# One transformer block with warped attention and two-of-eight experts on one core: ScalarE's distances in slices, another order of experts, transposes and norms, and another order of the first loads

## The reference

```python
mod = (silu(c) @ wmod).reshape(16, 6, 1, 128)           # sa, ca, ga, sb, cb, gb
ga, gb = (2*(g >= 0) - 1) * maximum(abs(g), 0.25)       # for g = ga and gb
h = layernorm(x) * (1 + ca) + sa
wave = silu(h @ wave_w.T + wave_b)                      # 2 x 8 values a row
freq  = mean(sigmoid(wave[0])) * 15 + 1                 # one a row
phase = mean(tanh(wave[1])) * 16
w = silu(h @ kernel_w.T + kernel_b)[..., :33]           # 8 heads x 33 taps
pos = clip(row + (tap - 16) * freq + phase, 0, 255)
g = h at floor(pos), h at floor(pos) + 1, interpolated  # 8 heads x 16 values
x = x + ga * silu(sum(g * w over taps) @ out_w.T)
h = layernorm(x) * (1 + cb) + sb
mask = the two largest of h @ router_w.T + router_b     # of 8 experts
x = x + gb * sum over experts of mask * (h @ expert_w[e] + expert_b[e])
```

## Time and profile before

| | |
|---|---|
| device time, median of 3 runs | 381.81 us |
| lowest, highest | 379.74, 382.86 us |
| profiled execution, device time | 381.84 us |
| its span in the profile | 380.1 us |
| mean granted clock of TensorE | 0.847 |
| activation table loads | 1 |

### The profile page before, as it was taken

One profiled execution on the slowest core, in us unless ns is written; L12 is line 12 of the kernel. 1 busy time (PEld: TensorE's weight loads), 2 busy tenths in 40 slices (PEclk: granted clock), 3 DMA queues, 4 the chain that ended last, 5 costly groups with the idle time before them and its releaser, 6 DMA issues.

```text
span 380.1 us, 5110 instructions
## 1 busy us (share of the span) xinstructions
PE 276.8 (73%) x1720; PEld 189.1 (50%) x1720; DVE 278.9 (73%) x584; ACT 237.2 (62%) x650; POOL 50.3 (13%) x64
## 2 busy tenths in 40 slices
PE   7873861989188928887498919894798479679796
PEld 4333430756065427644375517543564366358474
DVE  6678956995589962999469964999199949950623
ACT  2557755777588557867677758856676646575301
POOL 5102004500320031000310031002100300001100
PEclk9955855599669986999599988999699969899689
DMA  6600000010003000130004000400013001200001
GB/s 220 162 1 1 2 0 0 0 57 1 1 2 125 2 0 1 48 93 2 0 1 141 0 0 2 131 10 2 0 25 116 0 3 47 94 0 2 28 0 41
DMA packets 11871, 12.91 MB, mean 34 GB/s; under 512 B 1139, under 2 KB 10694, under 8 KB 11078
## 3 DMA queue, kind: packets, MB, share of 16 engines
q1 hardware_dynamic: 11108, 12.05, 10.5%
q10 hardware_dynamic: 738, 0.55, 0.5%
HBM read 10.45 MB, written 2.15 MB: 33 GB/s over the span
## 4 chain that ended last, share of the span: by engine, by line
PE 48%; ACT 29%; issue 7%; DVE 7%; POOL 7%; DMA 1%; SPq 0%; ACTq 0%; POOLq 0%; DVEq 0%
PE pT L898 12%; PE pE L986 11%; PE pR L878 7%; ACT A L470 6%; ACT xn L378 5%; POOL rs L309 5%; ACT c L456 4%; PE pY L912 4%; ACT xn L352 4%; PE pY L922 2%; PE pR L873 2%; ACT hT L400 2%; DVE AT L723 2%; PE pX L938 2%; DVE T L691 2%
## 5 line engine op out<-in xcount | busy, mean ns | idle before, releaser
L898 PE MATMUL pT<-early,AT 128*128 128x128 f32 x512 | 79.1, 304 | 21.2 <-ACT A L470 13.2
L470 ACT ACTIVATE A<-pT 128x512 f32<-128x512 f32 x128 | 70.6, 595 | 21.8 <-PE pT L898 21.4
L691 DVE COPY_PREDICATED T<-mask,T 128x672 f32<-128x672 int16 (+11 forms) x54 | 82.8, 1533 | 1.0
L898 PEld LDWEIGHTS pT<-early,AT 128*128 128x128 f32 x512 | 61.7, 155 | 36.1 <-ACT A L470 24.1
L723 DVE TENSOR_TENSOR AT<-T,c 128x2064 f32<-128x2064 f32 x32 | 72.4, 2302 | 7.0 <-ACT c L459 6.9
L986 PE MATMUL pE<-hm,late 128*128 128x256 f32 x240 | 65.7, 434 | 0.0
L986 PEld LDWEIGHTS pE<-hm,late 128*128 128x128 f32 x240 | 51.5, 220 | 10.6 <-issue 1.3
L938 PE MATMUL pX<-early,xn 128*128 128x128 f32 x32 | 8.7, 416 | 58.3 <-ACT xn L378 58.3
L307 POOL TENSOR_SCALAR ve<-sq 128x4 f32<-128x4 f32 (+1 forms) x18 | 7.7, 426 | 300.5 <-ACT xn L352 294.3
L378 ACT ACTIVATE xn<-x,nm,rs 128x128 f32<-128x128 f32 x64 | 26.4, 480 | 31.5 <-POOL nm L311 31.5
L938 PEld LDWEIGHTS pX<-early,xn 128*128 128x128 f32 x32 | 5.4, 206 | 61.6 <-ACT xn L378 61.1
(11 more groups left out here) (131 smaller groups left out, 363.0 us busy)
## 6 DMA issues: line engine op xcount, KB each, us to landing
mkb<-mask_rows SPq DMA_DIRECT2D x6, 1024.0 KB, 5.2
x<-in_x SPq DMA_DIRECT2D x7, 256.0 KB, 7.5
out<-x SPq DMA_DIRECT2D x7, 256.0 KB, 5.0
late<-in_late SPq DMA_DIRECT2D x1, 592.0 KB, 5.3
mkb<-mask_rows SPq DMA_DIRECT2D x1, 512.0 KB, 5.2
wmod<-in_wmod ACTq DMA_DIRECT2D x1, 384.0 KB, 4.2
early<-in_early SPq DMA_DIRECT2D x1, 278.0 KB, 4.4
x<-in_x SPq DMA_DIRECT2D x2, 128.0 KB, 3.6
```

The lines of the kernel that those rows point to most:

```text
L470: nc.scalar.activation(A[b][:, m, 2 * j:2 * j + 2, :].rearrange("p h l -> p (h l)"), pT[k % 2][:, :], ACT.Copy).then_inc(a_A, 1)
L691: nc.vector.copy_predicated(rows[:, :, :, j0:j1], spread(mask[:, k, 0:w, j0:j1], [P, w, H, j1 - j0], 2), rows[:, :, :, j0 + (1 << bit):j1 ...
L898: ins = nc.tensor.transpose(pT[k % 2][:, c0:c0 + P], AT[:, 2 * b + i, 2 * j + a, m * P:(m + 1) * P], ident)
```

## The change

- **c in slices.** `front_c(n, r0, r1)` now issues the slices r0 to r1 of the six, each with its own increment of a_abs, and `front_fall` the fall. Slices 0, 1 and 2 stand ahead of `mid_ao`, of row 0 and of `mid_y`; slices 3 to 5 between rows 1 and 2; the fall between rows 2 and 3.
- **ScalarE's loop.** The A copies of the second image are ahead of `front_hT`. The rows are issued one by one. `stats2` is right behind `front_wave`, then `front_hs`, `front_u`, `norm2`, `back_h2T`, `stats1`.
- **TensorE's loop.** The first half of the second image's A transposes is ahead of `front_xT`. Row 0 is ahead of `mid_y`, row 1 ahead of `mid_gate`, rows 2 and 3 behind it. Both images' experts are ahead of `back_x2T`.
- **VectorE's loop.** `residual` is ahead of the second image's `masked`.
- **The tail.** `front_c(LAST)` is behind all A copies of unit 7 and its fall behind `mid_ao`; the first `masked` of unit 6 is ahead of `spread_out(LAST, 0)`; unit 6's experts of the first image are ahead of `mid_gate(LATE)`, those of the second directly behind `mid_y(LAST)`; norm2(LATE) is behind the gate of the last unit, norm2(LAST) ahead of back_mk(LATE).
- **The start.** The identity is a pack of its own, `first`. SP loads x of unit 0, first, proj, x of unit 1, early, bits, experts, and behind hT of unit 0 the x of unit 2, late, rb and the rest. wmod comes in two parts, chunks 0 and 1 and, behind ScalarE's silu, chunks 2 to 5. The modulation has two parts, both into pL: the second one's matmuls stand behind the rows of iteration -1, its VectorE steps and the gates at the end of iteration 0. The bias parts are made ahead of the wait for the identity. `expert_parts` stands in iteration -1 behind the statistics of unit 1, `selectors`, its last step, at the end of iteration 0.

The core of the diff:

```diff
             load_x(0)
+            sp.dma_start(packs["first"][:, :], t["first"]).then_inc(d_first, 16)
+            sp.dma_start(proj[:, 0:NW], t["proj"][:, 0:NW]).then_inc(d_proj, 16)
+            sp.dma_start(proj[:, NW:NW + H], t["proj"][:, NW:NW + H]).then_inc(d_proj, 16)
+            sp.dma_start(proj[:, NW + H:NW + 2 * H], t["proj"][:, NW + 32:NW + 40]).then_inc(d_proj, 16)
+            load_x(1)
             sp.dma_start(packs["early"][:, :], t["early"]).then_inc(d_early, 16)
             sp.dma_start(bits[:, :, :], t["bits"].rearrange("p (k j) -> p k j", j=NGRID)).then_inc(d_bits, 16)
-            load_x(1)
             sp.dma_start(packs["experts"][:, :], t["experts"]).then_inc(d_exp, 16)
+
+            sp.wait_ge(a_hT, 1)
+            load_x(2)
             sp.dma_start(packs["late"][:, :], t["late"]).then_inc(d_late, 16)
             sp.dma_start(rb[:, :], t["rb"].rearrange("(a e) -> a e", a=1).to_broadcast([P, E])).then_inc(d_late, 16)
-            for n in range(2, NU):
+            for n in range(3, NU):
                 load_x(n)
...
-            act.dma_start(wmod[:, :], t["wmod"]).then_inc(d_wmod, 16)
+            act.dma_start(wmod[:, 0:2 * C], t["wmod"][:, 0:2 * C]).then_inc(d_wmod[0], 16)
...
             nc.scalar.activation(scT[:, :], cT[:, :], ACT.Silu).then_inc(a_silc, 1)
-            act.dma_start(proj[:, 0:NW], t["proj"][:, 0:NW]).then_inc(d_proj, 16)
-            act.dma_start(proj[:, NW:NW + H], t["proj"][:, NW:NW + H]).then_inc(d_proj, 16)
-            act.dma_start(proj[:, NW + H:NW + 2 * H], t["proj"][:, NW + 32:NW + 40]).then_inc(d_proj, 16)
+            act.dma_start(wmod[:, 2 * C:6 * C], t["wmod"][:, 2 * C:6 * C]).then_inc(d_wmod[1], 16)
...
-            def front_c(n):
+            def front_c(n, r0, r1):
                 w = tiles(n)
-                act.wait_ge(v_near, n + 1)
-                if n > 0:
-                    act.wait_ge(v_mult, LT * before(n))
+                if r0 == 0:
+                    act.wait_ge(v_near, n + 1)
+                    if n > 0:
+                        act.wait_ge(v_mult, LT * before(n))
                 cells = c[:, 0:w, :].rearrange("p a (j r) -> p a j r", r=BLK)
-                for r in range(BLK):
-                    ins = nc.scalar.activation(cells[:, :, :, r], near[:, 0:w, :], ACT.Abs, bias=off[:, r:r + 1])
-                ins.then_inc(a_abs, 1)
-                act.wait_ge(a_abs, n + 1)
+                for r in range(r0, r1):
+                    nc.scalar.activation(cells[:, :, :, r], near[:, 0:w, :], ACT.Abs, bias=off[:, r:r + 1]).then_inc(a_abs, 1)
+
+            def front_fall(n):
+
+                w = tiles(n)
+                act.wait_ge(a_abs, BLK * (n + 1))
                 nc.scalar.activation(c[:, 0:w, :], c[:, 0:w, :], ACT.Relu, bias=1.0, scale=-1.0).then_inc(a_c, 1)
...
             for i in range(-2, LAST):
+                second(i, -1, mid_A, 1)
                 run(i, 1, front_hT)
-                second(i, -1, mid_A, 1)
+                run(i, 0, front_c, 0, 1)
                 run(i, -1, mid_ao)
+                run(i, 0, front_c, 1, 2)
+                run(i, 1, front_row, 0)
+                run(i, 0, front_c, 2, 3)
                 run(i, -1, mid_y)
                 run(i, -1, mid_gate)
-                run(i, 1, front_row, 0)
                 run(i, 1, front_row, 1)
+                run(i, 0, front_c, 3, BLK)
+                run(i, 1, front_row, 2)
+                run(i, 0, front_fall)
+                run(i, 1, front_row, 3)
                 run(i, 1, front_wave)
+                run(i, -1, stats2)
                 run(i, 1, front_hs)
-                run(i, 0, front_c)
-                run(i, -1, stats2)
+                run(i, 1, front_u)
                 run(i, -1, norm2)
-                run(i, 1, front_u)
                 run(i, -1, back_h2T)
                 run(i, 2, stats1)
                 run(i, -2, back_moe)
                 run(i, 0, mid_A, 0)
                 run(i, -1, back_mk)
                 run(i, 2, norm1)
-            mid_A(LATE, 1, (0,))
-            front_c(LAST)
-            mid_A(LATE, 1, (1,))
+            mid_A(LATE, 1)
+            front_c(LAST, 0, BLK)
             mid_ao(LATE)
+            front_fall(LAST)
             mid_y(LATE)
             mid_gate(LATE)
             mid_A(LAST, 0)
             stats2(LATE)
             mid_ao(LAST)
-            norm2(LATE)
             mid_y(LAST)
             mid_gate(LAST)
+            norm2(LATE)
             back_h2T(LATE)
             back_moe(LATE - 1)
             stats2(LAST)
+            norm2(LAST)
             back_mk(LATE)
-            norm2(LAST)
             back_h2T(LAST)
             back_mk(LAST)
...
             def projection_parts():
-                dve.wait_ge(d_early, 16)
                 dve.wait_ge(d_kb, 48)
                 dve.wait_ge(g_zero, 3)
-                parts_on_partitions(kbl[:, :], kbr[:, :], kbs, kbt, kbp[:, :], ident[0:NP, 0:NP], v_kbp)
+                parts_of(kbl[:, :], kbr[:, :], kbs, v_kbp)
+
+            def projection_rows():
+                dve.wait_ge(d_first, 16)
+                on_partitions(kbs, kbt, kbp[:, :], ident[0:NP, 0:NP], v_kbp)
...
+            def modulation(part):
+
+                ks = slice(0, 2) if part == 0 else slice(2, 6)
+                dve.wait_ge(t_mod, part + 1)
+                nc.vector.tensor_copy(modT[:, ks, :].rearrange("p k b -> p (k b)"),
+                                      pL[:, ks.start * B:ks.stop * B]).then_inc(v_modT, 1)
+                dve.wait_ge(v_modT, 2 * part + 1)
+                nc.vector.tensor_scalar(modT[:, 3 * part + 1, :], modT[:, 3 * part + 1, :], 1.0, None, ALU.add).then_inc(v_modT, 1)
...
-            for i in range(-2, LAST):
+            stats1(0)
+            projection_parts()
+            modulation(0)
+            projection_rows()
+            for i in range(-1, LAST):
                 run(i, 0, network, range(0, 2))
-                if i < 0:
-                    run(i, 2, stats1)
-                if i == -2:
-                    projection_parts()
-                    modulation()
-                    gates()
+                if i == -1:
+                    stats1(1)
+                    expert_parts()
                 run(i, 0, sum_ends)
                 run(i, 0, network, range(2, 4))
                 run(i, -2, masked, 0)
                 run(i, 0, network, range(4, 5))
+                run(i, -1, residual)
                 second(i, -2, masked, 1)
-                run(i, -1, residual)
                 run(i, 0, network, range(5, 6))
                 run(i, 1, line)
                 run(i, 1, ends_of)
                 run(i, 1, products)
                 run(i, -2, total)
                 if i == 0:
-                    expert_parts()
+                    modulation(1)
+                    gates()
...
             sum_ends(LAST)
+            masked(LATE - 1, 0)
             spread_out(LAST, 0)
-            masked(LATE - 1, 0)
             residual(LATE)
             masked(LATE - 1, 1)
...
+            def modulation(part, ks):
+                pe.wait_ge(d_wmod[part], 16)
+                for k in ks:
+                    ins = mm(pL[:, k * B:(k + 1) * B], wmod[:, k * C:(k + 1) * C], scT[:, :], start=True, stop=True)
+                ins.then_inc(t_mod, 1)
+
+            modulation(0, range(0, 2))
+            pe.wait_ge(d_first, 16)
...
             for i in range(-2, LAST):
+                second(i, -1, mid_A, 1, 0)
                 run(i, 1, front_xT)
-                second(i, -1, mid_A, 1, 0)
                 second(i, -1, mid_A, 1, 1)
                 second(i, -1, mid_attend, 1, 0)
                 second(i, -1, mid_attend, 1, 1)
+                run(i, 1, front_row, 0)
                 run(i, -1, mid_y)
-                run(i, 1, front_row, 0)
+                run(i, 1, front_row, 1)
                 run(i, -1, mid_gate)
-                run(i, 1, front_row, 1)
+                run(i, 1, front_row, 2, 3)
+                if i == -1:
+                    modulation(1, range(2, 6))
                 run(i, 1, front_hb)
                 if i == -1:
                     warm_up(9)
                 run(i, -2, back_experts, 0)
+                second(i, -2, back_experts, 1)
                 run(i, -1, back_x2T)
-                second(i, -2, back_experts, 1)
                 run(i, -1, back_logits)
                 run(i, 0, mid_A, 0, 0)
                 run(i, -2, back_out)
             mid_attend(LATE, 1, 0)
             mid_attend(LATE, 1, 1)
             mid_y(LATE)
+            back_experts(LATE - 1, 0)
             mid_gate(LATE)
             mid_A(LAST, 0, 0)
             mid_A(LAST, 0, 1)
             mid_attend(LAST, 0, 0)
             mid_attend(LAST, 0, 1)
-            back_experts(LATE - 1, 0)
             mid_y(LAST)
+            back_experts(LATE - 1, 1)
             back_x2T(LATE)
```

49 lines of the change are left out of this document (24 added, 25 removed).

## The result

The changed kernel takes 331.7 us (median of 4 runs, 330.22 to 334.54) beside 381.5 us for the kernel before on the same chip (379.74 to 382.86): a ratio of 0.871, interval 0.863 to 0.878. It is faster by 50 us. The profiled execution took 330.67 us, its span is 328.9 us, and its mean granted clock 0.886 where that of before is 0.847.

What follows compares the result with a forecast made beforehand. A ring of waits through ScalarE and TensorE, no single engine. Savings 21.2 (iterations 3 to 6), 4.9 (2), 5.5 (7), 7 (1), 1.7 (start), 2.1 (tail), 42.4 in all, off 381.8 gave 339 us; range 325 to 358.

Steps and rivals of the forecast that it cites:

- (a): Loop, second image's A copies ahead of hT, first A transposes ahead of xT: saves 1.0 us an iteration (0 to 1.3).
- (b): ScalarE's loop, c in slices and hs behind the statistics: aoT to statistics 10.71 to 7.5 us, gain 3.2 (2 to 3.9).
- (c): ScalarE's loop, u ahead of the second norm, inside its wait for GpSimd: gain 0.7 us an iteration (0.4 to 1.0).
- (d): TensorE's loop, both images' experts ahead of the x2 transposes, filling the 8.08 us hole: waits of 1.3 us go.
- (e): TensorE between x2 transposes and first A copies: pauses may bring half clock, costing 0.9 us an iteration (0 to 2.6).
- GpSimd caught by both AT products: Rival: second norm's power instruction held under VectorE's products, norm2 3.3 us later in five iterations; 356 us, chance 0.10.
- VectorE's floor: VectorE's own work, 33.4 us an iteration, below which no reordering of the other engines can go.
- Start: Loads, identity, bias and modulation reordered: 0.6 us from these edits, 1.7 together with iteration 0 (-1 to 3).
- Tail: After the loop: c out of the A copies, experts and last norm moved; saves 2.1 us in all (0 to 4).
- Slices that cost what they save: Rival: rows wait for slices of c and TensorE for rows, (a) and (b) give 1; 358 us, chance 0.08.
- Half clock all round the loop: Rival: TensorE at 1.2 GHz through the loop becomes the bound, 48.7 us an iteration; 426 us, chance 0.03.
- Clock and GpSimd both kind: Rival: no half clock in the loop and the second norm waits only for the experts; 329 us, chance 0.17.

Runs made afterwards that it cites:

- e6: Kernel after with hT and the x transposes again ahead of the second image's A copies and transposes; 339.5 us, 0.899.
- e4: Kernel after with c whole (six slices and the fall) behind the tanh values, ahead of the second norm's statistics; 359.2 us, 0.950.
- e5: Kernel after with u behind the second norm again; 334.4 us, 0.886.
- e1: Kernel before with one edit, both images' experts ahead of the x2 transposes; 378.5 us, 0.998.
- e3: Kernel after with the second image's experts behind the x2 transposes again; 343.8 us, 0.910.
- e7: Kernel after with unused matmuls on zeros in TensorE's pauses, up to four ahead of the logits, eight ahead of the second pair of A transposes; 326.5 us, 0.863.
- e10: Kernel after with the tail of the kernel before on all three engines; 331.2 us, 0.875.
- e8: Kernel after with the first norm's sums ahead of h2T on ScalarE, the squares behind it; 325.5 us, 0.860.
- e9: Kernel after with one added wait: VectorE begins an iteration's first AT product only after GpSimd's three second-norm steps; 325.7 us, 0.859.
- e2: Kernel before with c cut into three pieces of two slices, its fall behind the second row; 363.5 us beside 378.9.
- e12: Kernel after with first-norm sums ahead of h2T, four zero-matmul fills per pause from unit 3, and VectorE's AT products waiting for GpSimd; 320.2 us, 0.846.
- e11: Kernel after with the loads, modulation, bias and expert parts of the kernel before; 333.5 us, 0.882.

## Why the prediction was right, and where its sizes were off

The mechanism and the sign held, and 331.7 lies in the range of 325 to 358. The forecast of 339 was 7 us too slow; in the profiled executions -42.4 was forecast and -51.2 came. The missing 8.8 lie in iterations 3 to 6 (5.6), start (2.3), tail (1.4), iterations 7 (0.8) and 1 (0.5), less iteration 2 (1.8 the other way). Of a full iteration, 5.3 was forecast and 6.56 came in iteration 5, whose parts can be read off and ScalarE's rows above:

**(a) 1.0.** From the end of the first image's attention to aoT's start it is 8.41 before and 7.12 after: 1.3. e6 takes the part away and loses 1.2. Right.

**(b) 3.2.** From aoT's start to the statistics' start 7.5 was forecast; it is 187.07 - 179.89 = 7.18, so 3.5. Right in size, and e4 shows a delay near it: 3.1 with c behind the tanh values.

**(c) 0.7: the step that failed.** From the statistics' start to h2T's start it is 9.12 before and 194.44 - 187.07 = 7.37 after: 1.75. The prediction left "the second norm's wait itself at 4 us". In iterations 3 to 5 there is none: the statistics come so early that all three GpSimd steps (1.59 us) begin before the AT products, and hs and u fill the time. What it put down as an upper case, "less than 4 us would give only 1.1 more", is what came, since x2T then waits for the experts (193.80, no pause): 1.05 more than the 0.7. The 0.7 itself did not come from where the text had it either: with the steps this early u's place is worth nothing in iterations 3 to 5 (e5), so that all 1.75 are the shorter wait. The likeliest value should have come from the order of starts, which the text had worked out itself ("ahead of the AT products by about the 1.5 us that the three steps want"), and not from the wait of before. The steps had that time: in iteration 5 the last one begins 0.08 us ahead of the products.

**(d) 1.3.** From h2T's start to the first A copy 6.22 is now 4.72: 1.5. Right in size. But e1 and e3 show that it has no value of its own: 0 in the old loop, 1.6 in the new. It is paid only when the norm no longer is what the x2 transposes wait for, and how much of the 1.6 is VectorE's later queue in e3 stays open.

**(e) the clock, -0.9.** From the first A copy to the attention's end it is 6.80 before and 8.31 after: -1.5. The place and the sign were right, the size was taken too small by 0.6; e7 measures what the clock is worth there, 1.6. The reason given, a pause like the 2.11 us at 326.39, is only half of it: in e10 a pause of the same 2.11 us was followed by full clock, in iteration 6 of the kernel after one of 0.95 by half, and in e8 pauses of 1.00 and 0.99 once by full and once by half. What decides, no run here shows.

That 5.3 lies within 1.3 of the 6.56 owes something to luck: (a) to (d) brought 8.05 where 6.2 was forecast, and the clock took back 1.5 where 0.9 was.

**Iteration 2**, 4.9 forecast, 3.1 came. Here the rival "GpSimd caught by both AT products" came true, in one iteration and not in five: the products start at 81.57, 0.08 us ahead of the first step (81.65). All three are held, and the norm waits 4.00 on top of hs and u, which stand in the wait now: it begins 8.02 us behind the statistics' start, where 5.89 of before were forecast to stay. With one image's experts VectorE has one masked product fewer and comes to the AT products sooner. e9 lets the steps pass and the iteration falls by 4.5; in e2 and e4 the same collision makes the difference between neighbouring iterations or adds to the loss. It was the prediction's sharpest rival by mechanism, and which of the two happens hangs on tenths of a microsecond.

**Iterations 1 and 7**, 7 and 5.5, came as 7.55 and 6.3. **VectorE's floor** of 33.4 was too high: it had counted all time outside its two long waits as work; busy it is 32.4 in iteration 5 after, and e8 and e12 have iterations of 31.86, with VectorE busy for 30.9 and 31.3 of it.

**Start**, 0.6 for its edits: e11 has 0.5, less than the 1.2 by which kernels with the same new start differ. With iteration 0 1.7 was forecast and 3.95 came; some 2.5 of these are the clock of the profiled execution of before, as e1 and e2, which start as before does, are at 38.6. So the two profiled executions differ by about 2.5 us that the change didn't make. Counting from 38.6, the start came in at 1.5. **Tail**, 2.1, for its order: 3.5 came, but 1.6 of them are full clock behind a pause where it was half before, which e10 has with the old order too. The other 1.9 match e10's difference and lie within the spread of kernels with one tail, so that the 2.1 is neither confirmed nor refuted. Whether the new loop or chance kept the clock there is open.

**The rivals.** Slices that cost what they save and no change are excluded by e2 and e4. Half clock all round the loop is excluded by the windows above. "Clock and GpSimd both kind" is half of what happened: GpSimd was kind in three of the four full iterations, the clock was not. The kernel came out between the forecast and that rival's 329, nearer to the latter.

## What to carry to other kernels

When a wait is to be shortened, work out its new length from the new order of starts, above all when it is for a small operation that another engine can hold: on which side of the big instruction it falls decided 4.5 us here. If the order is a matter of tenths, write it down as a wait (1.59 us spent on VectorE, 4.5 gained in iteration 2), and check that the engine which now waits doesn't become the bound. An edit in a ring has no value by itself: the experts' order was worth nothing before the norm was early, and 1.6 us an iteration on the mean once it was; and a hole that is filled with work may open another in which the clock falls, so the granted clock is to be read after every move.

## What the runs showed of the hardware that was not expected

- The length of a single pause did not tell TensorE's clock behind it. Half followed pauses of 2.29 us (199.79 in the kernel after), 0.95 (234.01) and 0.99 (e8, 193.79), full followed 1.00 (e8, 126.96), 0.94 (e9, 229.17) and 2.11 (e10, 277.40). With 1.89 us of fills on zeros in the pause the clock was full in iterations 3 to 6: 1.14 for the eight transposes of iteration 5.
- Fills cost more than they gave in iterations 1 and 2, where the clock was at half ahead of them: eight took 1.89 us at full and 3.62 at half (iteration 2), and the two iterations grew by 1.5 and 2.4.
- GpSimd's first step, on 128x4 elements, took 0.19 us alone, 2.27 under an AT product and 1.12 under a predicated copy of T (e3, 152.41; the copy runs from 151.75 to 153.52); its power instruction 1.01 alone, 2.95 to 3.15 under two products.
- Executions with one and the same start part by some 2.5 us by the clock alone: 41.09 us to the first attention before, with the rows of unit 1 at half clock, 38.63 and 38.60 in e1 and e2, with them at full.
